# Expert-weight store moved from the SyncE queue to the GpSimd queue, and the v-bias add cut into two halves

## The reference

```python
xn = layernorm(x)
# attention over the 16 heads of one token (not over tokens)
q  = xn @ Wq + bq                      # 1024 -> 1024
kv = (xn @ Wdown + bdown) @ Wup + bup  # 1024 -> 256 -> 2048
k, v = split(kv.reshape(B, T, 16, 128), 2)
q, k = rope(q), rope(k)                # same angle for all heads of a token
att = softmax(einsum('bthd,btgd->bthg', q, k) / 8)
a   = einsum('bthg,btgd->bthd', att, v).reshape(B, T, 1024) @ Wout + bout
# top-1 of 8 experts, each a 1024 x 1024 matrix
p = softmax(xn @ router_w.T + router_b)
e = argmax(p)
f = (xn @ expert_w[e].T + expert_b[e]) * max(p)
out = x + a + f
```

## Time and profile before

| | us |
|---|---|
| median of 3 runs (3103.77 to 3112.2) | 3106.15 |
| profiled execution, device time | 3099.09 |
| its span on the slowest core (core 4) | 3097.6 |
| spans of the other cores | 3078.0 to 3094.3 |

### The profile page before, as it was taken

The page is one execution under the profiler, slowest core; times in us unless marked ns, Lnnn a source line. Parts: engine busy times, 40 slices in busy tenths (PEclk is TensorE's granted clock), DMA queues, the critical chain, the costliest instruction groups (busy, mean ns, idle before and its releaser), DMA issues.

```text
span 3097.6 us, 38858 instructions; the slowest of 8 cores (3078.0 to 3097.6 us)
## 1 busy us (share of the span) xinstructions
PE 1958.5 (63%) x16622; PEld 1579.9 (51%) x16622; DVE 859.0 (28%) x1025; ACT 558.5 (18%) x770; POOL 102.4 (3%) x202
## 2 busy tenths in 40 slices
PE   0111157677676768586767667677758676676767
PEld 0011146556465647474656556565647465555546
DVE  2111123232324131322323232323232232423241
ACT  0111122120303030212112120303030211212030
POOL 0000000000000000000000000000000000000000
PEclk9855568778787869696878777786969687787868
DMA  4344433324151505151423324150515142332413
GB/s 161 126 161 162 154 118 137 109 101 145 55 190 36 184 27 191 55 189 56 164 82 131 115 89 157 55 189 16 180 51 190 55 163 83 112 134 74 158 40 138
DMA packets 60797, 366.44 MB, mean 118 GB/s; under 512 B 7107, under 2 KB 8131, under 8 KB 26580
## 3 DMA queue, kind: packets, MB, share of 16 engines
q1 hardware_dynamic: 32980, 196.19, 18.7%
q0 software_dynamic: 27648, 167.78, 14.6%
HBM read 330.39 MB, written 33.55 MB: 117 GB/s over the span
## 4 chain that ended last, share of the span: by engine, by line
PE 55%; DMA 17%; DVE 10%; ACT 8%; issue 4%; DVEq 3%; ACTq 2%; SPq 1%; POOL 0%; POOLq 0%
PE psb L777 24%; DMA exbuf<-exscratch 9%; PE psb L728 6%; DMA y_f<-exw 6%; PE psb L693 5%; PE psb L829 4%; PE psa L685 4%; ACT koct L552 2%; ACT vdm L557 2%; PE psb L674 2%; ACTq L483 2%; PE psa L716 2%; PE psa L842 2%; DVE exbuf L292 1%; DVEq L209 1%
## 5 line engine op out<-in xcount | busy, mean ns | idle before, releaser
L777 PE MATMUL psb<-xe,exbuf 128*128 128x256 bf16 x8192 | 962.0, 282 | 130.3 <-DVE xe L454 68.9
L777 PEld LDWEIGHTS psb<-xe,exbuf 128*128 128x128 bf16 x8192 | 822.4, 101 | 272.9 <-issue 155.3
L728 PE MATMUL psb<-lat,wup_sb 128*128 128x256 bf16 x1024 | 191.4, 366 | 122.9 <-ACTq L483 122.9
L454 DVE TENSOR_TENSOR xe<-xnf,mrep 128x2048 bf16<-128x2048 bf16 x96 | 116.2, 1224 | 453.9 <-PE psb L777 450.1
L728 PEld LDWEIGHTS psb<-lat,wup_sb 128*128 128x128 bf16 x1024 | 125.9, 127 | 188.4 <-issue 148.4
L659 PE MATMUL psa<-idbf,exbuf 128*128 128x128 bf16 x512 | 49.4, 278 | 262.7 <-DVE exbuf L292 259.5
L659 PEld LDWEIGHTS psa<-idbf,exbuf 128*128 128x128 bf16 x512 | 45.8, 129 | 266.2 <-issue 265.6
L685 PE MATMUL psa<-rT_sb,xnf 128*128 128x8 f32 x512 | 111.5, 361 | 79.0 <-DVEq L209 79.0
L685 PEld LDWEIGHTS psa<-rT_sb,xnf 128*128 128x128 f32 x512 | 110.4, 332 | 84.4 <-issue 84.4
L693 PE MATMUL psb<-xnf,wq_sb 128*128 128x256 bf16 x1024 | 153.0, 326 | 0.0
L674 PE MATMUL psb<-id,xn_t 128*128 128x128 f32 x256 | 57.6, 418 | 149.0 <-ACTq L483 149.0
(11 more groups left out here) (122 smaller groups left out, 1664.1 us busy)
## 6 DMA issues: line engine op xcount, KB each, us to landing
exbuf<-exscratch SPq DMA_DIRECT2D x128, 1024.0 KB, 5.6
exbuf<-exscratch POOLq DMA_DIRECT2D x128, 1024.0 KB, 8.5
y_f<-exw SPq DMA_DIRECT2D x64, 512.0 KB
x_t<-x POOLq DMA_DIRECT2D x32, 512.0 KB, 6.3
exscratch<-exbuf SPq DMA_DIRECT2D x8, 2048.0 KB, 8.6
out<-outsb POOLq DMA_DIRECT2D x32, 512.0 KB, 8.1
y_f<-wq SPq DMA_DIRECT2D x8, 512.0 KB
y_f<-wo SPq DMA_DIRECT2D x8, 512.0 KB
```

Of the source, the lines that this page charges most:

```text
L454: vector.tensor_tensor(out=re(xe[:, 2048 * (ex_i % 2):2048 * (ex_i % 2) + 2048], "p (cc t) -> p cc t", t=256), in0=src0, in1=m1.broadcast_ ...
L728: li = tensor.matmul(out=psb[:, 256 * gch:256 * (gch + 1)], lhsT=wup[:, 4096 * k + 128 * ch: 4096 * k + 128 * (ch + 1)], rhs=lat[:, 256 * ...
L777: li = tensor.matmul(out=pout(m), lhsT=exbuf[:, eb + 1024 * k + 128 * m: eb + 1024 * k + 128 * (m + 1)], rhs=xe[:, xb + 256 * k:xb + 256 * ...
```

## The change

There are two parts. First, the eight stores `exscratch<-exbuf` leave SyncE's program and stand in GpSimd's, behind the loads of the first two x tiles and ahead of everything that GpSimd does in the main loop, with the same waits. With them goes the point at which SyncE waited for ScalarE. VectorE's first cast of a round now waits for all 64 transposes of the round before (`4 + 8 * ex`, where it was two steps short of that). Second, the v-bias add is made in two instructions of 2048 columns with a drain and a semaphore step behind each (slots `vb0`, `vb1`); TensorE waits for `vb0` before the first v transpose and for `vb1` before the second.

```diff
-V_SLOTS = [..., 'qkb', 'vb',
-           'xe0', 'xe1', ...]
+V_SLOTS = [..., 'qkb', 'vb0',
+           'vb1', 'xe0', 'xe1', ...]
@@ gpsimd
                     xload(1)
+            for ex in range(8):
+                gpsimd.wait_ge(smS, 1 + 8 * (ex + 1))
+                if ex > 0:
+                    gpsimd.wait_ge(sexp, 16 * ex)
+                gdma(exs_d[ex], exbuf[:, 8192:16384], sexp)
+            if not phase0_only:
                 for i in range(nt):
@@ vector
                     if sr == 0 and ex > 0:
-                        vector.wait_ge(smT, 2 + 8 * ex)
+                        vector.wait_ge(smT, 4 + 8 * ex)
@@ vector
-                v3 = re(vdm[:], "p (oj g) -> p oj g", g=16)
-                vector.tensor_tensor(out=v3, in0=v3,
-                                     in1=vpatb[:].unsqueeze(1).broadcast_to([64, 256, 16]),
-                                     op=ALU.add)
-                vector.drain()
-                vinc()
+                for w in range(2):
+                    v3 = re(vdm[:, 2048 * w:2048 * (w + 1)], "p (oj g) -> p oj g", g=16)
+                    vector.tensor_tensor(
+                        out=v3, in0=v3,
+                        in1=vpatb[:].unsqueeze(1).broadcast_to([64, 128, 16]),
+                        op=ALU.add)
+                    vector.drain()
+                    vinc()
@@ tensor
-                tensor.wait_ge(smV, vv(i, 'vb'))
+                tensor.wait_ge(smV, vv(i, 'vb0'))
@@ tensor
                 tensor.wait_ge(smS, sv(i, 'extr0'))
+                tensor.wait_ge(smV, vv(i, 'vb1'))
@@ sync
-                sync.wait_ge(smS, 1 + 8 * (ex + 1))
-                if ex > 0:
-                    sync.wait_ge(sexp, 16 * ex)
-                dma(exs_d[ex], exbuf[:, 8192:16384], sem=sexp)
```

More of the change, by code:

```diff
@@ L20 @@
            'vst0', 'extr0', 'vst1', 'exp0', 'extr1', 'exp1', 'of0', 'of1']
-V_SLOTS = ['stats', 'negb', 'xnev', 'lgev', 'router', 'indwev', 'mrep', 'qkb', 'vb',
-           'xe0', 'xe1', 'sm0', 'sct0', 'pav0', 'sm1', 'sct1', 'pav1', 'yev', 'yadd']
+V_SLOTS = ['stats', 'negb', 'xnev', 'lgev', 'router', 'indwev', 'mrep', 'qkb', 'vb0',
+           'vb1', 'xe0', 'xe1', 'sm0', 'sct0', 'pav0', 'sm1', 'sct1', 'pav1', 'yev',
+           'yadd']
 T_PER, S_PER, V_PER = len(T_SLOTS), len(S_SLOTS), len(V_SLOTS)
```

## The result

The changed kernel takes 3025.24 us (median of 8 runs, 3019.87 to 3032.68) against 3105.71 us of the kernel before on the same chips: a ratio of 0.974, 95% interval 0.9722 to 0.9758. That is 80.5 us less. The forecast was 87.6 us less, 3018 us, with a range of 3000 to 3042.

What follows compares the result with a forecast made beforehand. Expert loads held behind SyncE's wait for the store bound phase 0, and TensorE's wait for the v-bias add the main loop; 70 + 17.6 = 87.6 us saved, giving 3018 us, range 3000 to 3042.

Steps and rivals of the forecast that it cites:

- The early load: Phase 0: with the store off SyncE, a round's first cast comes at T+8.2, rounds of 26.7 us plus d, not 39.73.
- T: Start of the fourth cast of an expert round in phase 0, from which the forecast counts times in us.
- The delay d: Phase 0: us a round by which the store slows loads beside it; bounded 0 to 5.8, computed 2.6, taken as 3.
- The rule of turns: Phase 0: queues taking turns by packet leave d at 2.6, saving 73 us; first come, first served would give nearer 80.
- The port: Phase 0: a store issue drifting into a VectorE cast that takes the shared port would start 1.2 us late.
- The seven rounds: Phase 0: seven rounds each save 13.0 - 3 us, 70 us in all; the eighth has no load behind it.
- The half add: Main loop, v-bias add: TensorE's first v transpose begins 1.1 us earlier in each of 16 tiles, 17.6 us in all.
- The whole store on the loads: Rival, phase 0: the store delays the loads by all its DMA time, d = 5.8; 3038 us, chance 0.14.
- the store is free: Rival, phase 0: the store falls wholly into gaps between loads, d = 0; 2997 us, chance 0.08.
- The half add buys nothing: Rival, main loop: a ScalarE copy or the clock's steps set the attention part's pace; 3036 us, chance 0.08.
- loads stay held: Rival, phase 0: VectorE's count or the staging buffer holds SyncE's loads, rounds stay at 39.7; 3088 us, chance 0.02.
- the slower case: Rival, phase 0: ScalarE's first copy waits for a late store, from a landing of 34 us; 3147 at 40, chance 0.03.

Runs made afterwards that it cites:

- the kernel with its stores last: The changed kernel with all eight stores issued by GpSimd at the end of phase 0, ScalarE's wait for them left out: 2996.7 us, ratio 0.9639.
- the wait order: The changed kernel with TensorE's waits ahead of the two v transposes reordered and two always-met waits left out: 3023.9 us, ratio 0.9712.

## Why the prediction was right

**The early load.** Right as worked out. The first cast moved from T+21.4 to T+8.2 and TensorE is what it waits for; the kernel with its stores last measured the base at 26.8 where the sum had 26.7.

**The delay d.** This is the term that was mis-sized: "I take 3" against 3.8 measured, 0.8 x 7 = 6 us of the 7 by which the seven rounds were off (70 against 63). The step counted 2.9 us of transfer for a load and 5.8 for the store, let store and load share the engines equally, found 2.6 and added 0.4 for a second queue's overhead.

What the transfers take alone, from first byte to last, show two windows: of the kernel before (one load) and of the kernel with its stores last (one store, issued at 322.86). Columns: length, engines' busy us, clock, DMA share, GB/s.

```profile
187.50:191.00 3.50, 0.00 (x0) 0.00 (x0) 0.00 (x0) 0.00 (x0) 0.00 (x0) 0.50 0.83 298
```

```profile
323.90:329.10 5.20, 3.39 (x16) 3.28 (x16) 0.00 (x0) 1.65 (x2) 0.00 (x0) 0.50 0.95 403
```

So a load takes 3.5 us and not 2.9, the store 5.2 and not 5.8 (which I had counted from the load's issue, 0.42 us behind the store's). The errors nearly cancel: two loads and a store are 12.2 us by these times, 11.6 by mine. Together they take longer. Two windows, of the kernel before (store and one load in one queue) and of the changed kernel (two loads and the store in two, core 0):

```profile
175.00:184.85 9.85, 0.00 (x0) 0.00 (x0) 0.00 (x0) 0.00 (x0) 0.00 (x0) 0.50 0.97 319
```

```profile
162.50:175.50 13.00, 0.00 (x0) 0.00 (x0) 1.23 (x1) 0.00 (x0) 0.54 (x1) 0.50 0.95 321
```

That is 9.85 us where the parts alone sum to 8.7, and 13.0 where they sum to 12.2. The excess of about 1 us is there in one queue as in two, so it needs no second queue, and GpSimd's way of issuing does not make it: from ScalarE's queue d was 4.3 (31.1 - 26.8). Nor did the two queues share the engines equally. The same round by queue (as above, q0 GpSimd's, q1 SyncE's; the store was issued at 162.87), in 162.5 to 166, 166 to 171 and 171 to 175.5:

```profile
q1 hardware_dynamic: 242, 0.93, 93.3%
...
q0 software_dynamic: 119, 1.95, 108.1%
q1 hardware_dynamic: 46, 0.12, 6.9%
...
q1 hardware_dynamic: 282, 1.03, 60.1%
q0 software_dynamic: 25, 0.15, 14.6%
```

The second load moves nearly all of its 1 MB before the store moves any. Then the store moves 1.95 of its 2.1 MB, and the third load, issued when the second cast ended at 168.56, gets going at about 171. Here they pass one after the other, in the order of issue. An estimate from the times alone: in a row from T+10.3 (162.5), the three end at T+22.5, and with 0.6 from last byte to cast the third cast stands at T+23.1, where it is at T+20.5 without a store. That is 2.6 us late, the sum's number again; the other 1.2 us of d goes with that excess, whose cause no run isolates. So the 2.6 held as a count of bytes, and the "overhead" of 0.4, a guess without a row, should have been 1.2. Where the delay falls was wrong too: 2.0 on the second load and 0.6 on the third in the step, 1.3 and 2.3 in the runs, since the load issued first mostly keeps the engines. The forecast that the third cast would be almost unchanged failed with it.

**The rule of turns.** The prediction weighed the Trainium skill's rule (DMA: Bandwidth & Descriptors, Queues, rings and completion order: the engines take turns between queues, packet by packet) against first come, first served. With one load out the round above shows the second: the store's queue moved nothing for the 3.1 us from its issue to 166, where a store alone starts about 1 us behind its issue (322.86 to 323.9 above). Whether its descriptors were ready for a turn in that time the trace does not show. With two staging buffers and more than one load out the queues do take turns, 100 packets beside 118, but not in equal bytes; there the trace agrees with the rule. The prediction's "nearer to 80" did not follow from first come, first served: whoever goes first, the same bytes have to pass before the third cast, and its own 2.6 comes out either way.

**The port.** The stores were issued at T+10.7, 0.5 later than put down but between casts, so the Trainium skill's rule on VectorE's copies and GpSimd's descriptors (SBUF — State Buffer, SBUF: two separate sides) met no case in which to act.

**The seven rounds.** 7 x (39.7 - 30.7) = 63 us instead of 70.

**The half add.** Forecast 17.6; the waits show 17.7 less at the first transpose and 1.8 more at the second, 15.9. In the timeline (columns as in rows 10) the halves are as worked out:

```profile
400.80 1.22 DVE L398 TENSOR_TENSOR vdm<-vdm,vpatb 64x2048 bf16<-64x2048 bf16 x1 [5.80 <-ACTq L492]
402.18 1.22 DVE L398 TENSOR_TENSOR vdm<-vdm,vpatb 64x2048 bf16<-64x2048 bf16 x1 [0.17 <-issue]
...
402.45 1.01 PE L747 MATMUL psa<-idbf,vdm 64*128 64x64 bf16 x16 [3.73 <-DVEq L216]
...
410.27 1.01 PE L763 MATMUL psa<-idbf,vdm 64*128 64x64 bf16 x16 [2.71 <-ACTq L492]
```

A half takes 1.22 us, near the upper bound of 1.23, and TensorE starts 1.65 us after it began, where 2.73 had gone by before. The 0.1 us at L763 I had called "unchanged"; it is the extra wait instruction, as the wait order showed.

**Sum.** 63 + 15.9 = 79 us from the traces, 80.5 measured, 87.6 forecast. The path was right in both parts; of the 8.8 us too many against the traces, 6 are d and 1.7 the second transpose's wait.

**The rivals.** "The whole store on the loads" (d = 5.8) and "the store is free" (d = 0) are both out at 3.8, though d lies nearer to the first. "The half add buys nothing" and "loads stay held" are out by the waits and the rounds. The late store of the slower case landed after 9.8 us where 34 was its threshold.

## What to carry to other kernels

When one queue issues both a load and a store that waits for a slower engine, look at what the load really needs: here only a free staging buffer. The store in the loads' queue cost 12.8 us a round beyond one without it, and 3.8 in a queue of its own. Take such a change in two terms: the order, read off the timeline and good to 0.1 us here, and the bytes side by side, each transfer at the time that it takes alone, in the order of issue. The second was too low here: it gave 2.6 where 3.8 was measured. Once the order is right, fill the stretches in which no DMA is out: a second staging buffer and a store in halves, with the new wait order, gave almost as much again as the change itself (77 us beside 80).

## What the runs showed that I had not expected

- A 2 MB store lands in 6.7 us alone on GpSimd's queue (stores last), 8.6 ahead of a load in one queue, 9.8 to 11.3 beside single loads, and 14.2 beside two staged loads. The transfer issued later pays: in the changed kernel's round above 3 us passed from the store's issue to its first byte.
- Beside a single load the store waited for the load issued ahead of it. With a load queued behind that one (two staging buffers) the queues took turns by packets, with four times the bytes for the store.
- ScalarE's queue was no better than GpSimd's for it, 12.5 us against 9.8 to 11.3, with rounds 0.4 us longer, though its issue takes 0.33 us instead of 0.54.
- A semaphore wait of TensorE that has long been met adds about 0.1 us when it is the last before the instruction.
